# Cross-attention (mLSTM) and FP4 feed-forward on one core: the transposed ctx taken from a host-made copy instead of being turned on the chip

## The reference, cut to what matters

```python
def _mlstm_forward(q, k, v, ...):          # called with q = layernorm(x), k = v = ctx
    x = concatenate([q, k, v]);  ig = x @ Wi + bi;  fg = x @ Wf + bf
    log_D = cumulated log_sigmoid(fg) differences + ig, lower triangle
    D = exp(log_D - max);  C = (qh @ kh.T / sqrt(dh)) * D
    h = (C / normalizer) @ vh;  return headwise layernorm(h) * ln_scale
...
x = x + _L0_xattn_ref(_layernorm(x), ctx_2048, ctx_2048, Wi, bi, Wf, bf, ln_scale)
x = x + _L0_ffn_ref(_layernorm(x), gate_up_packed, gate_up_scales, down_packed, down_scales)
# ffn: h = silu(x @ Wg.T) * (x @ Wu.T);  y = h @ Wd.T;  y / rms(y)
```

## Time and profile before

| | us |
|---|---|
| median of 3 runs (lowest, highest) | 674.09 (673.83, 675.59) |
| the profiled execution: its own time | 675.82 |
| the profiled execution: span from first to last instruction | 674.1 |
| TensorE matmul busy | 562.7 (83%) |
| VectorE busy | 486.1 (72%) |
| ScalarE busy | 298.2 (44%) |
| GpSimd busy | 310.1 (46%) |
| mean granted TensorE clock | 0.90 of full |

### The profile page before, as it was taken

How to read it: one execution, slowest core, us unless ns; L and a number is a source line. 1 busy time by engine, 2 the same in 40 slices (tenths; PEclk the granted TensorE clock), 3 DMA queues, 4 the chain that set the end, 5 groups by cost and what they waited for, 6 DMA issues and landing times.

```text
span 674.1 us, 7156 instructions
## 1 busy us (share of the span) xinstructions
PE 562.7 (83%) x2254; PEld 298.2 (44%) x2254; DVE 486.1 (72%) x805; ACT 298.2 (44%) x646; POOL 310.1 (46%) x310
## 2 busy tenths in 40 slices
PE   3648698549898897889898896989898897999997
PEld 2326467235464443434554443435464444333443
DVE  4997967987856789756877698836867796189601
ACT  3163446246645531237646612246655611177300
POOL 4222224517635574306746564307646563188600
PEclk9856778959977999899989998889989998999999
DMA  8052011027000110027200110046000000110000
GB/s 218 0 196 87 33 62 64 0 83 263 33 0 1 62 64 0 32 59 271 79 1 0 63 63 0 33 139 237 32 1 0 1 0 1 61 65 0 1 31 32
DMA packets 20880, 39.92 MB, mean 59 GB/s; under 512 B 7274, under 2 KB 7914, under 8 KB 20330
## 3 DMA queue, kind: packets, MB, share of 16 engines
q1 hardware_dynamic: 20842, 39.46, 16.9%
HBM read 30.93 MB, written 4.33 MB: 52 GB/s over the span
## 4 chain that ended last, share of the span: by engine, by line
DVE 41%; PE 27%; issue 15%; POOL 7%; ACT 6%; DMA 2%; SPq 1%; DVEq 0%; POOLq 0%; ACTq 0%
PE pf L887 8%; PE pf L875 6%; DVE ffn L1171 5%; PE pq L788 5%; DVE q_diag L1021 4%; POOL ffn L495 4%; PE po L817 4%; DVE ffn L1175 4%; DVE th L1184 3%; DVE tok L1135 3%; DVE bst L983 2%; ACT ffn L627 2%; ACT dmat L593 2%; DVE hT L1215 2%; DVE dmat L1077 2%
## 5 line engine op out<-in xcount | busy, mean ns | idle before, releaser
L875 PE MATMUL pf<-yT,gu_val 128*128 128x512 f16 x544 | 149.0, 396 | 28.7 <-DVE ffn L1171 17.6
L495 POOL TENSOR_TENSOR ffn<-ffn 128x512 f32<-128x512 f32 x88 | 115.4, 1313 | 118.8 <-ACT ffn L627 118.6
L887 PE MATMUL pf<-w_down,hT 128*128 128x512 f32 x352 | 156.6, 605 | 0.0
L627 ACT ACTIVATE ffn<-pf,gu_scale 128x512 f32<-128x512 f32 x136 | 86.4, 684 | 98.3 <-PE pf L875 72.4
L887 PEld LDWEIGHTS pf<-w_down,hT 128*128 128x128 f32 x352 | 67.9, 194 | 84.5 <-issue 83.4
L875 PEld LDWEIGHTS pf<-yT,gu_val 128*128 128x128 f16 x544 | 47.8, 101 | 108.2 <-DVE ffn L1175 35.0
L593 ACT ACTIVATE dmat<-negm,aT 128x128 f32<-128x128 f32 x256 | 78.1, 396 | 7.0 <-DMA negm<-negm_dram 7.0
L460 POOL TENSOR_SCALAR_AFFINE_SELECT dmat<-dmat 128x512 f32<-128x512 f32 x64 | 45.9, 740 | 69.2 <-ACT dmat L593 69.2
L817 PEld LDWEIGHTS po<-v_sb,dmat 128*128 128x128 f32 x512 | 69.5, 211 | 9.1 <-issue 5.7
L788 PE MATMUL pq<-q_diag,xT 128*128 128x512 f32 x128 | 69.7, 671 | 3.7 <-DVE dmat L1077 2.4
L1077 DVE SCALAR_TENSOR_TENSOR dmat<-pq,dmat 128x512 f32<-128x512 f32 x64 | 43.2, 685 | 35.0 <-PE pq L788 34.5
(11 more groups left out here) (122 smaller groups left out, 751.1 us busy)
## 6 DMA issues: line engine op xcount, KB each, us to landing
negm<-negm_dram SPq DMA_DIRECT2D x32, 512.0 KB, 5.6
ffn<-in_x SPq DMA_DIRECT2D x4, 1024.0 KB, 5.2
ctx_sb<-in_ctx SPq DMA_DIRECT2D x4, 1024.0 KB, 5.2
x_sb<-in_x SPq DMA_DIRECT2D x4, 1024.0 KB, 5.3
x_res<-x_sb SPq DMA_DIRECT2D x4, 1024.0 KB, 4.7
out<-x_res SPq DMA_DIRECT2D x16, 256.0 KB, 2.0
x_res<-in_L_ffn_gate_up_packed SPq DMA_DIRECT2D x1, 704.0 KB, 5.8
th<-in_L_ffn_down_packed SPq DMA_DIRECT2D x1, 352.0 KB, 6.3
```

Source lines behind the costliest of these rows:

```text
L495: pool.tensor_tensor(t, t, ffn[:, 2 * (h % 2) + 1], ALU.add).then_inc(tsum_ready, 1)
L627: act.activation(ffn[:, 2 * (h % 2) + g], bank(q, h, g), ACT.Copy, scale=gu_scale[:, g * GU + o:g * GU + o + 1]).then_inc(t_ready, 1)
L875: last = pe.matmul(bank(q, h, g), gu_val[:, h // 2 + h % 2 * FT, g], yT[:, part, g], start=(part == 0), stop=(part == 1))
L887: last = pe.matmul(pf[:, tt], hT[:, j, tt * P:(tt + 1) * P], w_down[:, j], start=(j == 0), stop=(j == FT - 1))
```

## The change

The host hands over a further input, `ctx_T`, which is ctx with its last two axes swapped. SyncE's queue loads it with four DMAs a pair into the ctx half of `xT` (1 MB a pair more; each run of memory is 256 float32, 1 KB). The 16 ctx transposes and four copies of each pair are gone, and `turn_x` and `read_xT` are one piece each, for x alone. `gate_sums` also waits for the new load. The load waits until the last scores of the pair before have read the tile. `load_ctx` no longer waits for the transposes.

```diff
+            def load_ctxT(p):
+                if not (isinstance(p, int) and p == 0):
+                    sp.wait_ge(qk_done, BLKS * UNITS * p)
+                for k in range(KT):
+                    sp.dma_start(xT[:, KT + k].rearrange("q (b s) -> q b s", b=2), ctxT_pairs[p][:, k]
+                                 ).then_inc(s_ctxT, 16)
...
                     if n is not None:
                         load_ctx(n)
+                        load_ctxT(n)
...
             load_xg(0, None)
             load_ctx(0)
+            load_ctxT(0)
             for i, w in enumerate((Wi, Wf)):
                 sp.dma_start(w_gate[:, :, i * DH:i * DH + NH], w.rearrange("(k q) h -> q k h", q=P)
...
-                if n is not None:
-                    turn_x(n, 0)
                 if p is not None and q is not None:
                     turn_y(p)
                 if n is not None:
-                    turn_x(n, 1)
+                    turn_x(n)
                     gate_sums(n)
...
             def gate_sums(p):
-                pe.wait_ge(xT_read, 2 * KT * (p + 1))
+                pe.wait_ge(xT_read, KT * (p + 1))
+                pe.wait_ge(s_ctxT, 16 * KT * (p + 1))
...
+    inputs = dict(inputs, ctx_T=_np.asarray(inputs["ctx_2048"]).transpose(0, 2, 1))
```

More of the change, by code:

```diff
@@ L68 @@
 SPARE = 19
-TURNS = (*range(KT, 2 * KT), *range(KT))
 PARTS = ((0, 1), (2,), (3,))
@@ L103, in link, with xattn_ffn @@
         self.wait()
-def xattn_ffn(nc, x, ctx, Wi, bi, Wf, bf, ln_scale, gu_packed, gu_scales, dn_packed, dn_scales, out):
+def xattn_ffn(nc, x, ctx, ctxT, Wi, bi, Wf, bf, ln_scale, gu_packed, gu_scales, dn_packed, dn_scales, out):
     x_pairs = x.rearrange("(p b) (c q) d -> p q (b c) d", b=2, q=P)
     ctx_pairs = ctx.rearrange("(p b) (c q) d -> p q (b c) d", b=2, q=P)
+    ctxT_pairs = ctxT.rearrange("(p b) (k q) s -> p q k b s", b=2, q=P)
     out_pairs = out.rearrange("(p b) (c q) d -> p q (b c) d", b=2, q=P)
@@ L219, in xattn_ffn @@
         s_ctx = sem("s_ctx")
+        s_ctxT = sem("s_ctxT")
         s_res = sem("s_res")
@@ L551, in _, with read_xT @@
             chain = Chain(act, act_g)
[L553 to L556, removed]
+            def read_xT(p):
+                for m in range(KT):
+                    act.wait_ge(xT_done, KT * p + m + 1)
                     if m == 0 and not (isinstance(p, int) and p == 0):
@@ L560, in read_xT @@
                         act.wait_ge(pv_done, UNITS * p)
-                    act.activation(xT[:, n], pq[:, m % 2], ACT.Copy).then_inc(xT_read, 1)
+                    act.activation(xT[:, m], pq[:, m % 2], ACT.Copy).then_inc(xT_read, 1)
             def softplus(p):
@@ L690, in iteration @@
                     down(q, 1)
-                if n is not None:
-                    read_xT(n, 0)
                 if p is not None and q is not None:
@@ L695, in iteration @@
                 if n is not None:
-                    read_xT(n, 1)
+                    read_xT(n)
                     softplus(n)
@@ L706, in iteration @@
                     down(q, 3)
-            read_xT(0, 0)
-            read_xT(0, 1)
+            read_xT(0)
             read_scales()
@@ L723, in _, with turn_x @@
         def _(pe):
-            def turn_x(p, half):
+            def turn_x(p):
                 first = isinstance(p, int) and p <= 1
[L727 to L738, removed]
+                pe.wait_ge(xn_ready, p + 1)
+                if not (isinstance(p, int) and p == 0):
+                    pe.wait_ge(prod_done, 2 * UNITS * p)
+                    pe.wait_ge(later_ready, UNITS * p)
+                if not first:
+                    pe.wait_ge(t_ready, 4 * FT * (p - 1))
+                for m in range(KT):
                     if m >= 2:
-                        pe.wait_ge(xT_read, 2 * KT * p + m - 1)
+                        pe.wait_ge(xT_read, KT * p + m - 1)
                     for tt in range(TT):
-                        c = slice((n % KT) * P, (n % KT + 1) * P)
-                        src = xg[:, tt, c] if n < KT else ctx_sb[:, tt, c]
-                        last = pe.transpose(pq[:, m % 2, tt * P:(tt + 1) * P], src, ident[:])
+                        last = pe.transpose(pq[:, m % 2, tt * P:(tt + 1) * P], xg[:, tt, m * P:(m + 1) * P],
+                                            ident[:])
                     last.then_inc(xT_done, 1)
             def gate_sums(p):
-                pe.wait_ge(xT_read, 2 * KT * (p + 1))
+                pe.wait_ge(xT_read, KT * (p + 1))
+                pe.wait_ge(s_ctxT, 16 * KT * (p + 1))
                 if isinstance(p, int) and p == 0:
@@ L828, in turn_y @@
                 if isinstance(p, int) and p == 0:
-                    pe.wait_ge(xT_read, 2 * KT * 2)
+                    pe.wait_ge(xT_read, KT * 2)
                 else:
@@ L852, in ffn_up @@
                 if spare(q, h) and h == 0:
-                    pe.wait_ge(xT_read, 2 * KT * (q + 2))
+                    pe.wait_ge(xT_read, KT * (q + 2))
                     pe.wait_ge(floor_ready, 2 * (q + 2))
@@ L964, in _ @@
             pe.wait_ge(const_ready, 6)
-            turn_x(0, 0)
-            turn_x(0, 1)
+            turn_x(0)
             gate_sums(0)
@@ L1012, in spread_q @@
             def spread_q(p, hg):
-                dve.wait_ge(xT_read, 2 * KT * p + KT + hg + 1)
+                dve.wait_ge(xT_read, KT * p + hg + 1)
                 if isinstance(p, int) and p == 0 and hg == 0:
@@ L1237, in prepare_down @@
                 if j < 4:
-                    dve.wait_ge(xT_done, 2 * KT)
+                    dve.wait_ge(xT_done, KT)
                     a, bb = (bits[:, k * KT * DW:(k + 1) * KT * DW].rearrange("q (o w) -> q o w", o=KT)
@@ L1334, in _ @@
             iteration(None, PAIRS - 1, None)
-_INS = ["x", "ctx_2048", "L0_xattn_Wi", "L0_xattn_bi", "L0_xattn_Wf", "L0_xattn_bf", "L0_xattn_ln_scale",
+_INS = ["x", "ctx_2048", "ctx_T", "L0_xattn_Wi", "L0_xattn_bi", "L0_xattn_Wf", "L0_xattn_bf", "L0_xattn_ln_scale",
         "L0_ffn_gate_up_packed", "L0_ffn_gate_up_scales", "L0_ffn_down_packed", "L0_ffn_down_scales"]
```

2 lines of the change are left out of this document (removed).

## The result

The changed kernel took 680.30 us in the median of four executions (679.99 to 681.81), the kernel before 674.13 beside it: 6.2 us more, a ratio of 1.0091 with an interval of 1.0062 to 1.0119. The forecast was 677.2 and the range ended at 680.0. Twelve and again twelve further executions, each set beside the kernel before on the same chip, gave ratios of 1.0017 (0.9979 to 1.0054) and 1.0019 (0.9987 to 1.0052), intervals that contain no change. So there are two things to explain: why it is slower, and why the first measurement showed three times the difference of the later ones.

A forecast was written before the change was run, and what follows sets the result against it. In the first 17.6 us the DMA queue was taken to bound the kernel; the boundaries waited on VectorE, not TensorE. Terms: 0 at three boundaries, +3.1 at the start, added to 674.09, forecast 677.2 us; range 674.2 to 680.0.

The forecast's parts named there:

- The three boundaries: Boundaries of pairs 1, 2 and 3: removing the ctx transposes gains 0, since TensorE waits or the reader comes later.
- the later loads: ctx_T loads for pairs 1 to 3: land well before the gate sums need them, cost 0.
- The hole in the DMA activity: Rival, at the start: nearly empty DMA time from 9 us hides the new load; 674.1 if all hidden, chance 0.18.
- TensorE was not the bound: Rival, at the boundaries: TensorE bounds after all, so removed transposes win 8.7 us, giving 668.5; chance 0.03.
- The term of the start: Start: the packed words land 3.1 us later behind 1 MB more, and VectorE's decoding starts that much later.
- One sign that the prediction named: Stretch from 20 to 100 us: a length other than before would show the prediction wrong.
- TensorE's busy time fall by 12 us: Whole kernel, expected sign: TensorE's busy time falls by about 12 us with nothing gained.
- clock luck: Rival, TensorE from 80 to 91 us: full clock returns there, winning 5.3 us, giving 671.9; chance 0.06.
- The idle hole cools TensorE: Rival, hole before turning y: half clock lasts through the gate sums; 682.2 for one boundary, 687 for two; chance 0.06.

The follow-up runs named there:

- e6: Changed kernel with ctx_T loaded for pair 0 only, no such loads for pairs 1 to 3: mean 677.6 +- 1.1 us.
- e2: Kernel before, transposes kept, plus an unread 1 MB ctx_T load at the start in 1 KB runs: mean 676.9 +- 0.6 us, together with e7.
- e7: Like e2, but the unread 1 MB at the start is ctx in 2 KB runs: mean 676.9 +- 0.6 us, both together.
- the hybrid: Changed kernel with pair 0 as before (transposes and copies, no ctx_T load at the start), later pairs from ctx_T: mean 676.4 +- 0.7 us.
- e11: The hybrid with idle TensorE products filling the holes at the boundaries of pairs 1, 2 and 3: mean 680.8 +- 1.0 us.
- e8: First twelve executions of the hybrid: 1.9 +- 1.1 us above the kernel before on the same chip.
- e5: Changed kernel unaltered, twelve more executions: mean 677.3 us.
- e13: Second twelve executions of the hybrid: 0.2 +- 1.1 us below the kernel before on the same chip.
- e15: Changed kernel unaltered, a further twelve executions: mean 678.1 us.
- e4: Changed kernel with 16 unread ctx transposes put back on TensorE at the boundaries of pairs 2 and 3: mean 675.7 us.
- e14: The hybrid with 16 unread ctx transposes put back on TensorE at the boundaries of pairs 1, 2 and 3: mean 675.8 +- 1.2 us.
- e16: Repetition of e4, the changed kernel with unread transposes at the boundaries of pairs 2 and 3: mean 677.5 us.
- e1: Changed kernel with pair 0's ctx_T load issued behind the packed words instead of ahead of the gate weights: mean 676.4 +- 0.9 us.

## Why the prediction was wrong

**What held.** The three boundaries are worth nothing: the y transposes start when VectorE's norm lets them, the gate sums end before their reader, and the later loads are hidden (e6 shows no cost, within 1.3 us). The start is where the change costs. The hole in the DMA activity did not hide the load, the queue's stall moved behind it. TensorE was not the bound.

**The term of the start.** It was set at 3.1 us, by the rule that each microsecond of the words is a microsecond of all that follows. The words did land 3.0 to 3.6 us later, but only 1.3 to 2.1 us of that reached the first mark, since the first decoding steps were faster. I took the decoding as a block of fixed length, and didn't look at whether its steps had the same duration throughout. By the mean of e2 and e7 the term is 1.2 +- 0.6. One sign that the prediction named for its being wrong came about here: the stretch from 20 to 100 us had another length, as the lag fell from 3.6 us at the first decoding step to 1.8 at 97 us. Nor did TensorE's busy time fall by 12 us; it fell by 3.4. But this term was too large, so it is not what took the first measurement above the range.

**The step that failed.** It was the sentence against clock luck, "three runs of before, each with its own luck, lie within 1.8 us". From it I took that the clock's falls move the time by about a microsecond, so the sum has the clock at nothing, the rival has luck only as a gain, and the range ends at 680.0. The 133 executions of before span 14 us, with a standard deviation of 3. The profile of the first measurement has 2.1 us of start and 4.8 us by which two falls in iteration 2 lengthened it, of which later stages gave back 1. Against the later means its 6.2 us are 2.0 of the change, 2.6 by which its four executions lie above the 677.7 of the changed kernel, and 1.6 by which the four beside them lie below the 675.7 of before. Why the executions of that first measurement were so alike, within 1.8 us on either side, and those on the later chips not, stays open. The rival also had the price too high: in the stretch from 79.39 to 88.07 us of before, which it named, only the hybrid's profile and e11's got part of the full level back, and e8 gained 1.3 us there for 5 us less at half clock, where half of it would be 2.5.

**Luck in the forecast.** That 677.2 lies near the later mean of 677.7 is luck in part. It stands on a median of three, 674.09, that was 1.6 us below the mean of before, and adds a term that was 1.9 too large by the mean of e2 and e7.

**The rival that had something in it.** "The idle hole cools TensorE" had 0.06 and was priced through the gate sums. These did not become late; at pair 1 they took 2.1 us longer, in slack. What the runs show is more diffuse: by the rows of the table, kernels without the boundary transposes have 132 to 134 us at half clock (e5, e6, e8, e13, e15), those with them 124 to 126 (before, e2 to e4, e7, e14, e16), a difference of 9 us with an error under 2; e1, which lacks them, had 126 +- 3 and doesn't fit, and with it the difference is 7.6 +- 1.5. The profiles show where it lies. The boundary of pair 2, from the last `state` product of iteration 1 to the first of iteration 2, with the unread transposes (e4) and without (e15):

```profile
223.21:308.80 85.59, 73.50 (x252) 34.94 (x251) 64.59 (x112) 30.95 (x63) 38.31 (x36) 0.96 0.24 85
...
223.05:308.77 85.72, 71.96 (x236) 33.16 (x235) 64.58 (x112) 30.96 (x63) 38.27 (x36) 0.94 0.23 77
```

That is 6.8 against 10.3 us at half clock in stretches of the same length to 0.13 us. Over the three boundary stretches together, seven profiles without the transposes (after, e1, e5, e6, e8, e13, e15) have 50 us at half clock in the mean and seven with them 44, and the stretches last 220.8 and 220.5 us, a difference of 0.3 +- 0.3. So the missing transposes do go with more time at half clock, most of it stands at the boundaries, and there it costs next to nothing. The totals leave room for a little more: e13 and e8 against before give 0.7 +- 0.8, e5 and e15 against e4 and e16 give 1.2 +- 0.9, weighted together 0.9 +- 0.6 us, which is not shown.

So the change costs 2.0 +- 0.8 us: 1.2 +- 0.6 by the load ahead of the words, and 0.8 that may be the clock or nothing but scatter. Forecast were 3.1. The direction was right. The four executions of the first measurement gave three times the size, with an interval (1.0062 to 1.0119) that leaves out the later one, 1.003: such an interval holds only the scatter within one measurement.

No kernel here beats the one before. The best of those with ctx_T, the hybrid with or without the unread transposes and e1, are not distinguishable from it.

## What to carry to other kernels

A unit of work taken from the busiest engine is worth nothing where that engine waits anyway: look at what ends the idle time behind the removed work, not at busy shares. A load added at the start costs what is queued behind it; put it behind whatever the first long stage waits for, if its own reader has slack. And before a difference under 1% is explained, compare the mean clock of the executions: on this kernel 0.01 of mean clock, 13.5 us at half level, is 3.8 us.

## What the runs showed of the hardware that was not expected

- One program on one core spread from 668.9 to 683.3 us (133 executions), and the time at half clock accounts for most of it (correlation 0.92, 0.28 us per microsecond).
- The same stretch of iteration 2 took 35.58 us with one short fall and 40.42 us with two falls of 7 us, in e2 and in the changed kernel alike. TensorE was at 0.52 of full clock in the two falls while busy for 7.00 of 7.00 us, so being busy did not at once bring the full level back. At the boundary of pair 2, 3.5 us more at half clock changed the length by 0.13 us (e15 against e4).
- VectorE's integer steps took 1.25 us instead of 0.53 (e1, twice, and before, once) and 2.17 instead of 1.43 while GpSimd worked on a 128x512 tile beside them.
- The Trainium skill ("TensorE: Matmul & The Clock Gate", HAM oscillation) advises to avoid idle gaps. Here the products in the gap shortened the first transposes behind it (0.65 against 1.12 us), as that would have it, and the kernel became slower in the mean (681.5 us, against 676.6 for before on the same chip); why is open.
- 1 MB in runs of 1 KB and in runs of 2 KB delayed the words alike (20.50 and 20.62 us), though the 1 KB runs moved more slowly: about 350 GB/s in the slices from 8.1 to 10.4 us of the changed kernel, against 396 before for 2 KB. Its 40 slices from 9 to 20 us:

```profile
GB/s 346 350 350 350 346 354 265 225 161 141 138 113 59 19 5 0 0 45 82 209 201 108 182 124 212 171 256 283 290 281 257 222 221 216 224 229 257 270 233 189
```
